# Moving the late copies of row maxima, and the score units, in a transformer layer on one core

## The chip, the cores and the metric

One of the cores of a Trainium2 chip runs the whole program. The metric is the device time of one execution in microseconds (us), as a median over runs. The core has five engines that each work through their own list of instructions in order and wait for each other by semaphores: PE (TensorE, matrix products; PEld is its loading of weights), DVE (VectorE), ACT (ScalarE), POOL (GpSimd) and SP (SyncE, which here issues the DMAs).

## The reference

A layer over 4 batches of 512 tokens with 256 features: causal attention with 16 heads, and a gated feed forward with 1024 hidden features. Cut to what matters:

```python
qkv = layernorm(x) @ w_qkv.T + b_qkv            # q, k get a rotary embedding
attn = softmax(where(causal, -inf, q @ k.T * HEAD_DIM ** -0.5))
x = x + layernorm((attn @ v) @ w_out.T + b_out)
h = layernorm(x)
hidden = fwht(silu(h @ W1.T) * (h @ W3.T))      # Walsh-Hadamard transform
x = x + layernorm(hidden @ W2.T)
```

All is float32, and the kernel keeps nearly that precision: most products are made of three products of high and low halves.

## The kernel before, in words

The softmax needs the largest score of each query row before the exponential. So the scores are computed twice. In a first pass, **score units** (`score_unit` on PE, ACT, POOL and DVE) compute scores with queries on the partitions, for one tile of 128 queries (qt, 0 to 3) and as many heads as fit 512 columns. DVE (line 923) takes the maximum of each row. When all heads of a tile are done, ACT copies the maxima as their high half (line 688), POOL (`max_low`, line 811) makes the low half, a unit of kind "turn" lets PE transpose both (line 430), and ACT copies the rows into `q_t` (line 677), twice for each turn. There are 44 units of scores and 5 turns: units 0 to 41 run inside the feed forward of the batch before (for the first batch, ahead of everything), and the last 7, the **tail** (the last six heads of the last query tile, and their turn), run inside the attention of the batch itself.

In the second pass, `attend`, PE computes scores again with keys on the partitions (`score_t`, line 448, four matmuls for a head) and the maxima are subtracted in the same product. ACT takes the exponential of a head (`exps`, line 656, 128x1280), POOL zeroes the masked triangle (`cut`, lines 820 and 823), and PE multiplies with the values (`values`, line 464), four heads to a group, in four steps by key tile. `values(g, kt)` starts six heads behind `score_t`. In one pass of `attend`'s loop PE does `score_t(h)`, then the tail units that `TAIL_AFTER[h]` names, then a step of `values`. Heads and units are counted from 0 here.

Score units use the banks of `ps` in turn; in the feed forward these are banks 4 and 5, so a unit waits until the unit two places earlier has had its maxima taken, or, where that was a turn, until ACT has made both of its row copies. In the tail, units use banks 6 and 7; `values` of group 0 writes to bank 6 and of group 1 to bank 7.

The feed forward runs over 8 chunks of hidden features (a = 0 to 7). For each PE does four `up` products, ACT the silu (line 662), DVE the product with the second half (`gate`, line 1001), ACT the high half (`hid_high`, line 668), POOL the low half (`hid_low`, line 803), and PE four `down` products for the chunk before. `UNITS_AFTER` is a table with a row for each chunk: how many score units go between its ups, how many between the downs that follow, and how many ahead of the last chunk's downs (`gap`). Each engine goes through the same list of steps. Units that the table leaves over come behind the last down.

ACT needs another table of functions for exp than for silu. A one-element exponential (line 714) loads it ahead of time.

On POOL, the iteration of a batch is: `cut` of all 16 heads; behind head 5 (`ROOT_AFTER`) the reciprocal root for the next batch's layer norm (`root(b + 1, "x")`, line 779, which waits for DVE's statistics, line 879); and the `max_low` of the tail where the table says. DVE works through the six tail maxima, then the last subtractions of the batch before, and then the statistics of x for the next batch.

Of the kernel before, what the change touches and what calls it, by code (L numbers as in the profile page):

```python
# [30 lines left out]
ACT = mybir.ActivationFunctionType  # L31
# [7 lines left out]
HCH = HIDDEN // P  # L39
# [27 lines left out]
N_SCORES = len(UNITS)  # L67
# [4 lines left out]
TAIL_UNITS = range(N_UNITS, len(UNITS))  # L72
SCORE_NO = [sum(u[0] == "scores" for u in UNITS[:n]) for n in range(len(UNITS))]
TAIL_BANKS = [6 + n % 2 for n in range(TAIL)] + [7]
TAIL_AFTER = {4: (0, 2), 5: (2, 4), 6: (4, 6), 7: (6, 7)}


def turn_of(unit):
# [60 lines left out]

UNITS_AFTER = [(0, 0, 0), (3, 2, 0), (2, 3, 0), (4, 1, 0), (4, 2, 0), (4, 3, 0), (4, 3, 0), (4, 1, 0), (0, 0, 1)]
STEPS, EARLY_UNITS = feed_forward_steps(UNITS_AFTER)
STEPS_LAST, _ = feed_forward_steps(None)
UNIT_BANKS = unit_banks(EARLY_UNITS)
FIRST_UNIT_BANKS = [4 + n % 4 for n in range(N_UNITS - 1)] + [5] + TAIL_BANKS
# [13 lines left out]
def layer_kernel(nc, x, w_qkv, b_qkv, w_out, b_out, w1, w3, w2, rope, hadamard, eye, mask, selector, out):  # L160
    ctx = ExitStack()
    with ctx:
# [72 lines left out]
        minus_half = sb("minus_half", [P, TILES])  # L235
        spare = sb("spare", [P, 1])
# [135 lines left out]
        def _(pe):  # L372
# [79 lines left out]
            def values(b, g, kt):  # L452

                if kt == 0:
                    if g == 0:
                        pe.wait_ge(S["maxed"], (b + 1) * N_SCORES)
                    pe.wait_ge(S["masked"], b * HEADS + 4 * g + 4)
                    if g == 1:
                        pe.wait_ge(S["rows_in"], 2 * (b + 1) * N_TURNS)
                    if g >= 2:  # L460
                        pe.wait_ge(S["o_copied"], b * GROUPS + g - 1)
                for j in range(4):
                    h = 4 * g + j
                    ins = pe.matmul(ps[32 * j:32 * j + 32, 6 + g % 2, kt * P:TOKENS], v_t[:, kt, h, :],  # L464
                                    probs[:, h % PROBS, KEY_COL[kt]:KEY_COL[kt] + TOKENS - kt * P],
                                    start=(kt == 0), stop=(kt == TILES - 1), skip_group_check=True)
                if kt == TILES - 1:
                    ins.then_inc(S["pv_done"], 1)
# [158 lines left out]
        def _(act):  # L627
# [30 lines left out]
            def silu(b, a):  # L658
                act.wait_ge(S["up_done"], b * HCH + a + 1)
                if a >= 2:  # L660
                    act.wait_ge(S["hid_l"], b * HCH + a - 1)
                act.activation(gate[:, a % 2, :], bank(2 * (a % 2)), ACT.Silu).then_inc(S["silu_done"], 1)  # L662
# [44 lines left out]
            def feed_forward(b, steps):  # L707
                for kind, n, i in steps:
                    if kind == "up" and i == 3:
                        silu(b, n)  # L710
                    elif kind == "gate":
                        hid_high(b, n)
                        if n == HCH - 1:
                            act.activation(spare[:, :], minus_half[:, 0:1], ACT.Exp)
                    elif kind == "unit":
                        score_unit(b + 1, n, UNIT_BANKS)

# [37 lines left out]
            def iteration(b, order, steps):  # L755
                for h in range(HEADS):
                    exps(b, h)
                    for n in range(*TAIL_AFTER.get(h + 1, (0, 0))):
                        score_unit(b, TAIL_UNITS[n], UNIT_BANKS if b else FIRST_UNIT_BANKS)
                if order is MIX:  # L760
                    for t in range(TILES):
                        xt_high(b + 1, t)
                mix(b, order)
                feed_forward(b, steps)
# [8 lines left out]
        def _(pool):  # L773
# [32 lines left out]
            def max_low(b, n):  # L806
                turn = turn_of(UNITS[n])
                if turn is not None:
                    qt, first, stop = TURNS[turn]
                    pool.wait_ge(S["max_h"], b * N_TURNS + turn + 1)  # L810
                    pool.tensor_tensor(max_s[:, qt % 2, 1, first:stop], maxima[:, qt % 2, first:stop],
                                       max_s[:, qt % 2, 0, first:stop].bitcast(F32), ALU.subtract).then_inc(S["max_l"], 1)
# [13 lines left out]
            def iteration(b, order, steps):  # L826
                for h in range(HEADS):
                    cut(b, h)
                    for n in range(*TAIL_AFTER.get(h + 1, (0, 0))):
                        max_low(b, TAIL_UNITS[n])  # L830
                    if h == ROOT_AFTER and order is MIX:
                        root(b + 1, "x")
                for m in order:
                    if m[0] == "e":
                        rope_products(b + 1, int(m[1]))
                    elif m[0] in "vw":
                        root(b, {"v": "y", "w": "h"}[m[0]] + m[1])
                for kind, n, i in steps:
                    if kind == "gate":
                        hid_low(b, n)  # L840
                    elif kind == "unit":
                        max_low(b + 1, n)
                    elif kind == "ln_z":
                        root(b, "z%d" % i)
# [284 lines left out]
```

## Time and profile before

| | |
|---|---|
| median of 3 runs | 500.91 us (500.86 to 501.76) |
| the profiled execution, its own time | 497.78 us |
| its span in the profile | 496.1 us |
| PE busy with matmuls | 405.0 us (82% of the span) |
| DVE busy | 281.2 us (57%) |
| ACT busy | 210.9 us (43%) |
| POOL busy | 162.1 us (33%) |
| mean granted TensorE clock | 0.938 |

The four batches follow each other at some 107 us. Attention of the second batch runs from about 189 to 218 us in the span, then comes a mixed stage (output projection, normalisation, and q, k, v of the next batch), and the rest of the period is feed forward, with the score units of the next batch among it. PE is the busiest engine in all of them, so what counts is where PE waits.

### The profile page before, as it was taken

The numbers are of one execution on the slowest core, as the hardware profiler recorded it, in microseconds if no ns is written. First come the engines' busy times: TensorE is split into PE (matmuls) and PEld (weight loads), VectorE is DVE, ScalarE is ACT, GpSimd is POOL, SyncE is SP. The second block draws the span as 40 slices with busy tenths as digits, with TensorE's granted clock in tenths as the row PEclk, the third lists the DMA queues.
The fourth block names the chain that finished last, engine by engine and source line by source line (L and its number), as shares of the span: only waits on it lengthen the run. The fifth ranks groups of instructions, "written<-read, shape, count | busy, mean of one in ns | idle before, by whom it ended". The sixth has DMA issues, their size and how long they took to land.

```text
span 496.1 us, 7892 instructions
## 1 busy us (share of the span) xinstructions
PE 405.0 (82%) x2884; PEld 338.2 (68%) x2884; DVE 281.2 (57%) x936; ACT 210.9 (43%) x314; POOL 162.1 (33%) x284
## 2 busy tenths in 40 slices
PE   1679677999599997988599988987799979858992
PEld 1569645558489985557499975566699965448991
DVE  7554583625937776536856776267576754273114
ACT  4445234753323337843423347813332367423221
POOL 4136002533512226514422235614132245321232
PEclk9999865999969999999889999999799999997998
DMA  6549900000397000200695001102880002000001
GB/s 230 215 136 247 212 1 1 2 2 0 127 255 171 1 1 1 85 1 1 179 245 130 1 1 42 44 1 72 219 201 21 1 1 85 1 1 1 1 1 42
DMA packets 35463, 36.95 MB, mean 74 GB/s; under 512 B 2016, under 2 KB 34528, under 8 KB 35424
## 3 DMA queue, kind: packets, MB, share of 16 engines
q1 hardware_dynamic: 35424, 36.45, 26.6%
q8 instruction: 23, 0.38, 0.3%
q14 instruction: 16, 0.13, 0.1%
HBM read 21.76 MB, written 14.68 MB: 73 GB/s over the span
## 4 chain that ended last, share of the span: by engine, by line
PE 58%; DVE 13%; DMA 9%; issue 7%; ACT 6%; SPq 3%; POOL 2%; DVEq 0%; POOLq 0%; ACTq 0%
PE ps L266 30%; PE ps L448 8%; PE ps L464 7%; PE ps L436 5%; DMA qk_scratch<-qk_s 4%; DMA q_t<-qk_scratch 4%; ACT probs L656 4%; DVE masked_scores L923 2%; SPq L293 2%; DMA raw_bias<-in_b_out 2%; PE ps L498 2%; DVE xy L985 1%; POOL hid_s L803 1%; PE ps L405 1%; DVE stats_h L870 1%
## 5 line engine op out<-in xcount | busy, mean ns | idle before, releaser
L923 DVE CUSTOM_DVE_ANT_0 masked_scores<-ps,mask_row 128x128 bf16<-128x128 f32 (+3 forms) x256 | 114.4, 488 | 61.6 <-PE ps L436 61.1
L266 PE MATMUL ps<-xt,w_s 128*128 128x256 f32 x768 | 111.7, 294 | 0.0
L266 PEld LDWEIGHTS ps<-xt,w_s 128*128 128x128 f32 x768 | 106.2, 202 | 0.5
L803 POOL TENSOR_TENSOR hid_s<-gate,hid_s 128x512 fp32r<-128x512 f32 x32 | 41.2, 1287 | 135.9 <-ACT hid_s L668 135.9
L656 ACT ACTIVATE probs<-ps 128x1280 f32<-128x1280 f32 x64 | 76.4, 1242 | 9.5 <-PE ps L448 8.9
L436 PE MATMUL ps<-k_t,q_t 96*128 96x128 f32 (+3 forms) x256 | 71.7, 356 | 9.8 <-DMA q_t<-qk_scratch 5.6
L448 PEld LDWEIGHTS ps<-q_t,k_t 128*128 128x128 f32 x256 | 44.9, 198 | 32.2 <-ACT probs L656 14.7
L266 PE MATMUL ps<-w_s,hid_s 128*128 128x256 f32 x384 | 55.5, 284 | 7.0 <-POOL hid_s L803 7.0
L448 PE MATMUL ps<-q_t,k_t 128*128 128x512 f32 (+3 forms) x256 | 55.7, 345 | 5.6 <-ACT probs L656 4.0
L266 PEld LDWEIGHTS ps<-w_s,hid_s 128*128 128x128 f32 x384 | 51.6, 190 | 9.3 <-POOL hid_s L803 8.7
L436 PEld LDWEIGHTS ps<-k_t,q_t 96*128 96x128 f32 x256 | 43.0, 198 | 18.6 <-DVE maxima L923 10.9
L464 PE MATMUL ps<-probs,v_t 128*32 128x128 f32 (+3 forms) x512 | 43.6, 441 | 4.8 <-DVE maxima L923 3.9
L662 ACT ACTIVATE gate<-ps 128x512 f32<-128x512 f32 x32 | 19.1, 596 | 64.1 <-PE ps L266 64.0
L1001 DVE TENSOR_TENSOR gate<-gate,ps 128x512 f32<-128x512 f32 x32 | 21.9, 685 | 41.9 <-ACT gate L662 41.7
L266 PE MATMUL ps<-wqkv_s,q_t 128*128 128x512 f32 (+1 forms) x192 | 41.8, 356 | 3.6 <-DVE bias_s L1061 3.6
L820 POOL TENSOR_SCALAR_AFFINE_SELECT probs<-probs 128x384 f32<-128x384 f32 x64 | 33.8, 528 | 31.7 <-ACT probs L656 31.4
L797 POOL TENSOR_TENSOR rot_s<-qk_b,rope_t 128x256 f32<-128x256 f32 x32 | 25.7, 824 | 49.6 <-ACT qk_b L646 41.2
L930 DVE COPY o_t<-ps 128x512 f32<-128x512 f32 x16 | 11.1, 692 | 49.5 <-PE ps L464 49.0
L266 PEld LDWEIGHTS ps<-wqkv_s,q_t 128*128 128x128 f32 x192 | 32.3, 200 | 8.6 <-issue 4.0
L668 ACT ACTIVATE hid_s<-gate 128x512 fp32r<-128x512 f32 x32 | 20.2, 631 | 29.3 <-DVE gate L1001 29.3
L630 ACT ACTIVATE xt<-ps 128x256 fp32r<-128x256 f32 x32 | 12.0, 384 | 44.5 <-PE ps L507 33.0
L405 PE MATMUL ps<-ident,rot 128*128 128x128 f32 x64 | 11.6, 309 | 21.6 <-DVE rot L910 21.6
(99 smaller groups left out, 485.3 us busy)
## 6 DMA issues: line engine op xcount, KB each, us to landing
qk_scratch<-qk_s SPq DMA_DIRECT2D x32, 256.0 KB, 5.6
k_t<-qk_scratch SPq DMA_DIRECT2D x16, 384.0 KB, 5.5
q_t<-qk_scratch SPq DMA_DIRECT2D x8, 768.0 KB, 8.8
qk_scratch<-qk_s SPq DMA_DIRECT2D x8, 512.0 KB, 5.5
xa<-in_x SPq DMA_DIRECT2D x4, 512.0 KB, 9.6
xy<-in_x SPq DMA_DIRECT2D x4, 512.0 KB, 3.5
out<-xy SPq DMA_DIRECT2D x8, 256.0 KB, 2.3
o_t<-in_w SPq DMA_DIRECT2D x1, 1024.0 KB, 10.0
```

The costliest lines, as they stand in the source:

```text
L266: ins = eng.matmul(o, lhs(i), rhs(j), start=first and n == 0, stop=last and n == 2, skip_group_check=skip)
L436: ins = pe.matmul(o[:, i * keys:(i + 1) * keys], q_t[0:QK_ROWS, h // 2, qt * P:qt * P + P], k_t[0:QK_ROWS, h, 0:keys], start=(i == 0), sto ...
L448: ins = pe.matmul(ps[:, col // 512, col % 512:col % 512 + n], k_t[:, h, kt * P:kt * P + P], q_t[:, h // 2, kt * P:TOKENS], start=(kt != 3) ...
L464: ins = pe.matmul(ps[32 * j:32 * j + 32, 6 + g % 2, kt * P:TOKENS], v_t[:, kt, h, :], probs[:, h % PROBS, KEY_COL[kt]:KEY_COL[kt] + TOKENS ...
L656: act.activation(probs[:, h % PROBS, :], src, ACT.Exp, scale=SCALE).then_inc(S["exp_done"], 1)
L662: act.activation(gate[:, a % 2, :], bank(2 * (a % 2)), ACT.Silu).then_inc(S["silu_done"], 1)
L668: act.activation(hid_s[:, a % 2, 0, :], gate[:, a % 2, :], ACT.Copy).then_inc(S["hid_h"], 1)
L797: ins = pool.tensor_tensor(o[:, :, e, :], src[:, :, 1 - e, :], tab[:, 1, e, :].unsqueeze(1).broadcast_to([P, 2 * HEADS, HALF]), ALU.mult)
L803: pool.tensor_tensor(hid_s[:, a % 2, 1, :], gate[:, a % 2, :], hid_s[:, a % 2, 0, :].bitcast(F32), ALU.subtract).then_inc(S["hid_l"], 1)
L820: pool.affine_select(out=v, in_=v, compare_op=ALU.is_ge, fill=0.0, base=0, pattern=[[0, 3], [1, P]], channel_multiplier=-1)
L923: ins = dve.tensor_tensor_reduce(masked_scores[:, SCORE_NO[n] % 2, i * keys:(i + 1) * keys], ps[:, banks[n], i * keys:(i + 1) * keys], mas ...
L1001: dve.tensor_tensor(gate[:, n % 2, :], gate[:, n % 2, :], bank(2 * (n % 2) + 1), ALU.mult)\
```

## The change

Six edits belong together. On PE, the tail's turn goes from behind `score_t(7)` to behind `score_t(8)`. On ACT and POOL, the copy of the last six heads' maxima goes from behind head 5 to behind head 7, and ACT's copy of their rows from behind head 6 to behind head 8. `values` of group 0 waits for one maximum less: for five of the six tail units. In the feed forward, two units go from behind the last chunk's ups to the chunks before, and the turn of the first ten heads goes from behind the last down to ahead of the last chunk's downs. ACT loads its table for exp ahead of the last `hid_high`, not behind it.

```diff
-TAIL_AFTER = {4: (0, 2), 5: (2, 4), 6: (4, 6), 7: (6, 7)}
+TAIL_AFTER = {4: (0, 2), 5: (2, 4), 6: (4, 6), 8: (6, 7)}
+TAIL_COPY_AFTER = {7: 5, 8: 6}
...
-UNITS_AFTER = [(0, 0, 0), (3, 2, 0), (2, 3, 0), (4, 1, 0), (4, 2, 0), (4, 3, 0), (4, 3, 0), (4, 1, 0), (0, 0, 1)]
+UNITS_AFTER = [(0, 0, 0), (3, 2, 0), (2, 3, 0), (4, 1, 0), (4, 2, 0), (4, 4, 0), (4, 4, 0), (4, 0, 0), (0, 0, 1)]
...
                     if g == 0:
-                        pe.wait_ge(S["maxed"], (b + 1) * N_SCORES)
+                        pe.wait_ge(S["maxed"], (b + 1) * N_SCORES - 1)
...
                     if kind == "up" and i == 3:
                         silu(b, n)
+                        if n == HCH - 1:
+                            act.activation(spare[:, :], minus_half[:, 0:1], ACT.Exp)
                     elif kind == "gate":
                         hid_high(b, n)
-                        if n == HCH - 1:
-                            act.activation(spare[:, :], minus_half[:, 0:1], ACT.Exp)
...
                     exps(b, h)
-                    for n in range(*TAIL_AFTER.get(h + 1, (0, 0))):
-                        score_unit(b, TAIL_UNITS[n], UNIT_BANKS if b else FIRST_UNIT_BANKS)
+                    if h in TAIL_COPY_AFTER:
+                        score_unit(b, TAIL_UNITS[TAIL_COPY_AFTER[h]], UNIT_BANKS if b else FIRST_UNIT_BANKS)
...
                     cut(b, h)
-                    for n in range(*TAIL_AFTER.get(h + 1, (0, 0))):
-                        max_low(b, TAIL_UNITS[n])
+                    if h in TAIL_COPY_AFTER:
+                        max_low(b, TAIL_UNITS[TAIL_COPY_AFTER[h]])
```

The first place is POOL in the attention of the first batch. AFFINE_SELECT rows are `cut`, two for each head, rstd_x and shift_x are the root for the next batch, and max_s is `max_low` of the last six heads. Before, from the end of head 5's cut:

```order
L823 AFFINE_SELECT probs<-probs 128x128
L811 TENSOR_TENSOR max_s<-maxima,max_s 128x6
L779 TENSOR_TENSOR rstd_x<-mv_x,minus_half 128x4
L782 TENSOR_TENSOR shift_x<-mv_x,rstd_x 128x4
L820 AFFINE_SELECT probs<-probs 128x3x128
```

And in the changed kernel (its lines are one higher), from the same instruction:

```order
L824 AFFINE_SELECT probs<-probs 128x128
L780 TENSOR_TENSOR rstd_x<-mv_x,minus_half 128x4
L783 TENSOR_TENSOR shift_x<-mv_x,rstd_x 128x4
L821 AFFINE_SELECT probs<-probs 128x3x128
L824 AFFINE_SELECT probs<-probs 128x128
L821 AFFINE_SELECT probs<-probs 128x3x128
L824 AFFINE_SELECT probs<-probs 128x128
L812 TENSOR_TENSOR max_s<-maxima,max_s 128x6
```

`max_low` stood ahead of the root; now it stands behind it and behind the cuts of heads 6 and 7.

The second place is PE in the feed forward: the downs that follow the ups of chunk 6 (rows with hid_s), up to the first up of chunk 7. L436 is a score unit, L430 the turn of query tile 2 (unit 34). Before:

```order
L436 MATMUL ps<-k_t,q_t 128x512
L266 MATMUL ps<-w_s,hid_s 128x256 x6
L436 MATMUL ps<-k_t,q_t 128x512
L266 MATMUL ps<-w_s,hid_s 128x256 x3
L436 MATMUL ps<-k_t,q_t 128x512
L266 MATMUL ps<-w_s,hid_s 128x256 x3
L430 MATMUL ps<-ident_r,max_s 32x128
L266 MATMUL ps<-xt_65,w_s 128x256 x6
```

In the changed kernel:

```order
L437 MATMUL ps<-k_t,q_t 128x512
L267 MATMUL ps<-w_s,hid_s 128x256 x3
L437 MATMUL ps<-k_t,q_t 128x512
L267 MATMUL ps<-w_s,hid_s 128x256 x3
L431 MATMUL ps<-ident_r,max_s 32x128
L267 MATMUL ps<-w_s,hid_s 128x256 x3
L437 MATMUL ps<-k_t,q_t 128x512
L267 MATMUL ps<-w_s,hid_s 128x256 x3
L437 MATMUL ps<-k_t,q_t 128x512
L267 MATMUL ps<-xt_65,w_s 128x256 x6
```

The turn came last before the ups; now two units follow it, and the second of them (unit 36) uses the turn's bank.

The third place is ACT from the silu of chunk 7 to the first exponentials. Before:

```order
L662 ACTIVATE gate<-ps 128x512
L668 ACTIVATE hid_s<-gate 128x512
L714 ACT_TABLE_LOAD
L714 ACTIVATE spare<-minus_half 128x1
L688 ACTIVATE max_s<-maxima 128x10
L677 ACTIVATE q_t<-ps 32x128
L677 ACTIVATE q_t<-ps 32x4x128
L656 ACTIVATE probs<-ps 128x1280 x6
```

In the changed kernel:

```order
L663 ACTIVATE gate<-ps 128x512
L713 ACT_TABLE_LOAD
L713 ACTIVATE spare<-minus_half 128x1
L689 ACTIVATE max_s<-maxima 128x10
L669 ACTIVATE hid_s<-gate 128x512
L678 ACTIVATE q_t<-ps 32x128
L678 ACTIVATE q_t<-ps 32x4x128
L657 ACTIVATE probs<-ps 128x1280 x8
```

The table load and the copy of the first ten heads' maxima now stand between the silu and the last `hid_high`.

## Rows read from the trace of the kernel before

**Rows 1.** Timeline, second batch's attention: start us, us, engine, line, idle before.

```profile
198.28 0.08 DVE L923 DVE_READ_ACCUMULATOR2_ANT maxima<- 128x1 f32 x1
...
198.89 0.08 DVE L923 DVE_READ_ACCUMULATOR2_ANT maxima<- 128x1 f32 x1
...
199.03 1.07 PE L464 MATMUL ps<-probs,v_t 128*32 128x512 f32 x8 [0.98 <-DVE maxima L923]
...
201.90 1.01 POOL L779 TENSOR_TENSOR rstd_x<-mv_x,minus_half 128x4 f32<-128x4 f32 x1 [2.34 <-DVE mv_x L879]
...
202.44 0.64 PE L464 MATMUL ps<-probs,v_t 128*32 128x256 f32 x8
...
203.14 0.52 POOL L820 TENSOR_SCALAR_AFFINE_SELECT probs<-probs 128x384 f32<-128x384 f32 x1
...
204.59 0.53 POOL L820 TENSOR_SCALAR_AFFINE_SELECT probs<-probs 128x384 f32<-128x384 f32 x1
```

**Rows 2.** Timeline ahead of the first batch's attention: a low half, then its turn.

```profile
79.19 0.21 POOL L811 TENSOR_TENSOR max_s<-maxima,max_s 128x10 fp32r<-128x10 f32 x1 [5.89 <-ACT max_s L688]
...
79.55 0.27 PE L430 MATMUL ps<-ident_r,max_s 128*32 128x128 f32 x1 [2.22 <-POOL max_s L811]
```

**Rows 3.** Timeline, first batch's attention (94 to 96) and the last one's.

```profile
94.67 0.52 POOL L820 TENSOR_SCALAR_AFFINE_SELECT probs<-probs 128x384 f32<-128x384 f32 x1
...
95.03 0.64 PE L464 MATMUL ps<-probs,v_t 128*32 128x256 f32 x8
...
415.94 4.83 ACT L656 ACTIVATE probs<-ps 128x1280 f32<-128x1280 f32 x4
...
416.85 0.64 PE L464 MATMUL ps<-probs,v_t 128*32 128x256 f32 x8
...
417.34 0.52 POOL L820 TENSOR_SCALAR_AFFINE_SELECT probs<-probs 128x384 f32<-128x384 f32 x1 [1.66 <-ACT probs L656]
```

**Rows 4.** The chain that ended last, in order of time: start us, us, what.

```profile
173.06 0.18 PE ps L436
173.24 0.35 PE ps L266 x3
```

**Rows 5.** Timeline, feed forward of the first batch, chunks 5 to 7.

```profile
173.55 0.19 PEld L436 LDWEIGHTS ps<-k_t,q_t 96*128 96x128 f32 x1 [0.16 <-DVE maxima L923]
...
179.05 0.63 ACT L668 ACTIVATE hid_s<-gate 128x512 fp32r<-128x512 f32 x1 [0.97 <-DVE gate L1001]
...
179.75 0.94 PE L266 MATMUL ps<-xt,w_s 128*128 128x256 f32 x6
...
179.95 1.06 ACT L677 ACTIVATE q_t<-ps 32x128 fp32r<-32x128 f32 x2 [0.27 <-PE ps L430]
...
183.58 0.60 ACT L662 ACTIVATE gate<-ps 128x512 f32<-128x512 f32 x1 [2.56 <-PE ps L266]
...
185.15 0.63 ACT L668 ACTIVATE hid_s<-gate 128x512 fp32r<-128x512 f32 x1 [0.97 <-DVE gate L1001]
...
185.80 1.28 ACT L714 ACT_TABLE_LOAD   x1
...
187.18 1.68 PE L266 MATMUL ps<-w_s,hid_s 128*128 128x256 f32 x12 [1.49 <-POOL hid_s L803]
187.20 0.20 ACT L688 ACTIVATE max_s<-maxima 128x10 fp32r<-128x10 f32 x1
...
188.70 0.22 PE L430 MATMUL ps<-ident_r,max_s 128*32 128x128 f32 x1
...
189.28 1.50 PE L448 MATMUL ps<-q_t,k_t 128*128 128x512 f32 x8 [0.35 <-ACT q_t L677]
```

**Rows 6.** Timeline, last batch's feed forward, chunk 7.

```profile
484.53 0.63 ACT L668 ACTIVATE hid_s<-gate 128x512 fp32r<-128x512 f32 x1 [0.75 <-DVE gate L1001]
```

**Rows 7.** Stretches of the first mixed stage (busy by engine, PEclk, DMA), then PE's timeline.

```profile
134.00:136.00 2.00, 0.00 (x0) 0.00 (x0) 1.99 (x4) 1.72 (x3) 1.44 (x2) 0.65 0.56 195
...
136.22 1.11 PE L405 MATMUL ps<-ident,rot 128*128 128x128 f32 x4 [2.62 <-DVE rot L910]
```

## The prediction

> **What bounds the kernel now.** The page says that PE is the busiest engine (82% of the span), so I looked for the places where PE waits, in the timeline around each edit, and read from the chain which of those waits reach the end of the program. Two places matter: the middle of each attention, and the end of each feed forward.
>
> In the second batch's attention [rows 1] the reader is to see PE waiting 0.98 us at 199.03 for DVE's last tail maximum, which ends at 198.97, before `values(0,0)`. From there the chain runs on PE alone through the rest of the attention but for its last exponential: score products and value products follow each other without a gap. Whatever delays PE there delays the end by as much. The same rows show POOL: its root for the next batch waits for DVE's statistics until 201.90, takes 1.01, and `cut(6)` starts only at 203.14. `cut(6)` and `cut(7)` together take 1.45 (203.14 to 204.59). Before the change nobody cared: POOL had made the low half of the tail maxima ahead of the root.
>
> At the end of the feed forward [rows 5] PE waits 1.49 us for the low half of chunk 7 (187.18), behind silu, gate, high half and low half in a row. Then the turn of the first ten heads (188.70) and ACT's copy of its rows hold up the first `score_t` until 189.28.
>
> **The change, part by part.** *`values` wait for five of the six tail units.* The fifth unit's maximum is read at 198.28 + 0.08, the sixth's at 198.89 + 0.08 [rows 1]. PE starts `values(0,0)` 0.61 sooner, at 198.42. ACT no longer stands still for the maxima, so exponential 6 starts with its scores. That gives -0.6 per batch if nothing else comes in the way.
>
> *The tail's turn, its low half behind the root and two cuts.* POOL's list is now cut 5, root, cut 6, cut 7, `max_low`. The root's time is set by DVE's statistics, which DVE makes behind the sixth maximum, as before. So the cuts stay at 203.14 and `max_low` starts at 204.59. From the start of a `max_low` to its turn on PE it took 79.55 - 79.19 = 0.36 [rows 2]: the turn comes at 204.95. I allow 0.15 for the turn, so `values(0,2)`, which stands behind it in PE's list with everything after, starts at 205.10. Before it started at 202.44 [rows 1]. That is +2.66, with the 0.61 already in it: PE would be there at 198.42 + 3.41 = 201.83, and waits some 3.1 us. Behind PE's wait for the turn stand `values(0,2)`, `score_t(9)` and all later heads. ACT needs 4.83 us for four heads [rows 3] and is not what the chain runs over there, so it has nothing to give back.
>
> The first batch: `cut(6)` at 94.67 [rows 3], + 1.45 + 0.36 + 0.15 = 96.63 against 95.03: +1.6. The third batch has the pattern of the second: +2.7. The last batch has no root. There exponential 7 can start about 1.1 before its 415.94 (0.6 from the values, 0.5 since it no longer stands behind the row copies), its cut 1.40 later (417.34 - 415.94), then 0.8 for the cut, 0.36 and 0.15: 417.5 against 416.85 [rows 3], so +0.6. Sum for the attentions: 1.6 + 2.7 + 2.7 + 0.6 = +7.6. The row copies behind exponential 8 are made long before `score_t(10)` needs them; were that cover gone, they would cost their 0.5 us a batch.
>
> *Two units earlier in the feed forward.* They leave PE's idle stretch ahead of chunk 7's downs, where they cost nothing, for chunks 5 and 6, where PE has no gap. In chunk 5, unit 27 starts at 173.55 when DVE has freed its bank [rows 5], and will again, but now a down (0.35) and a unit (0.18) [rows 4] follow it: +0.5, and nearly 0.1 for a wider unit among the ups of chunk 6. In chunk 6, the turn of tile 2 came last before the ups. Now units 35 and 36 follow it and unit 36 uses its bank, so it waits for ACT's two row copies (1.06 us), which stand behind `hid_high(6)`: 179.05 + 0.6 + 0.63 + 1.06 = 181.3 [rows 5]. With the unit itself (0.24, estimated from the chain's other units) the ups of chunk 7 start at 181.6, not at 179.75: +1.85.
>
> *The exp table ahead of `hid_high(7)`.* From the load's start to ACT's next work it took 187.20 - 185.80 = 1.40 [rows 5]. Now that and the maxima's copy (0.2) stand between silu and `hid_high`. Before, 185.15 - (183.58 + 0.60) = 0.97 lay there, for the gate. So +0.6 on the chain to the downs. In the last batch there is no maxima's copy, and 0.75 lay there [rows 6]: +0.65, to the very end.
> The Trainium skill (ScalarE: Activation LUTs, "What ACT_TABLE_LOAD costs") has 1283 ns for the load, as here, and about 1380 ns for a drain besides. The row shows no such drain: the spare exponential and the next copy follow in 1.40 in all. By the page each of four moves would cost 1.4 more, 5.5 in the sum; by the row nothing. I take the row.
>
> *The turn of ten heads ahead of the downs.* It now falls into PE's idle stretch, and its row copies are done while the downs run. `score_t(0)` can start where the turn was, at about 188.65 instead of 189.28 [rows 5]: -0.65.
>
> Per feed forward with units (three): 1.85 + 0.6 - 0.65 = +1.8, in all +5.4.
>
> **Sum.** 7.6 + 5.4 + 0.65 = +13.6 us. Against the profiled execution's own 497.78 this gives 511.4; the median of the runs is 500.91, 3.1 above it, and I add to the median: 514.5. No transfer is on these paths; output and input DMAs shift with the batches.
>
> **The clock.** In the first mixed stage the granted clock fell from 1.0 (2.4 GHz) to 0.5 (1.2 GHz) in a stretch without PE work, 2.62 us idle before a matmul [rows 7]. PE's 1.49 us wait at 187.18 cost no clock. The new waits of about 3.1 us (second and third batch) lie near the first. I take it that one of the two brings such a fall, and price it at 1.6 us: some 3 us of work that PE bounds at half speed. Bounds: nothing, and 3.4 for a fall of double length. So 516 us.
>
> **Rivals.** (1) *The clock falls in most of the new gaps*: the attentions of three batches and the ends of three feed forwards, where PE's idle stretch grows from 1.5 to over 2.5. Six falls at 1.6 are 9.6, so 524. For it: gaps near 2.6. Against: PE's work stands close on both sides. Chance 0.12.
> (2) *The bank waits in the feed forward are hidden*: if chunk 6 doesn't wait for the row copies, its +1.85 shrinks to the two units, 0.5; -1.3 three times, and without the clock: 514.5 - 4 = 510.5. The waits are in the program by bank and order, so against it speaks all but the exact times. Chance 0.11.
> (3) *Faster.* The change wins if POOL reaches `max_low` before PE reaches the turn, so that no new wait comes. Then attention gains 0.6 four times, the early turn 0.65 three times, the table load costs 0.6 four times and the units 0.5 three times: near -0.5; with the load hidden too, -2.9, so 498. The place is POOL's root: it would have to start by 201.83 - 0.36 - 1.45 - 1.24 = 198.8; the row has 201.90, for statistics that DVE can't begin before the sixth maximum. Chance 0.04.
> (4) *No change*: the delays are taken up by slack behind them. PE is the chain to the end of each attention. Chance 0.03.
> (5) *A drain at each table load*, as worked out above from 1.4 four times: with the rest, 521.5. Ruled out nearly by 187.20 - 185.80. Chance 0.03.
> The forecast keeps 0.67.
>
> **How the numbers follow.** The forecast's own range is 512 to 519 (clock from nothing to three falls, and 2 us of error over seven terms). To hold 8 in 10 it is stretched toward (2) and part of (1): 509.5 to 521. Within 0.2% (1 us) is about what a measurement can't tell from no change. Slower: 0.67 + 0.12 + 0.11 + 0.03 = 0.93; same 0.03; faster 0.04.
>
> **What the profile after would show.** Right: PE's turn in the attention of batches two and three with an idle time near 3 us before it, released by POOL's `max_s`, about 2 in the first and 1 in the last; POOL's `max_s` of 128x6 behind the second cut after the root; `values(0,0)` with an idle time of some 0.4; a wait of unit 36 on ACT's `q_t` of 0.5 us or more in chunk 6; ACT's table load directly behind the silu, with `hid_high(7)` about 2.1 behind silu's start; `score_t(0)` directly behind the last downs. Wrong: `max_s` done before PE gets to the turn; a root that doesn't wait for statistics; or a drop of the granted clock in each attention.

## The result, and the profile after

| | before | changed |
|---|---|---|
| median of 4 runs | 500.88 us | 520.32 us (518.13 to 522.08) |
| ratio, 95% interval | | 1.0394 (1.0338 to 1.0451) |
| span of the profiled execution | 496.1 us | 519.3 us |
| mean granted TensorE clock | 0.938 | 0.921 |

The changed kernel is 19.4 us slower; 516 was forecast, within 509.5 to 521. Run again beside other kernels (below) it was 18.2 us slower (517.22 against 499.01, ratio 1.0356, 1.0316 to 1.0396).

The first view is the timeline of the changed kernel in the second batch's attention, the place of [rows 1]:

```profile
204.86 0.08 DVE L924 DVE_READ_ACCUMULATOR2_ANT maxima<- 128x1 f32 x1
...
205.00 1.07 PE L465 MATMUL ps<-probs,v_t 128*32 128x512 f32 x8 [0.38 <-DVE maxima L924]
...
208.50 1.01 POOL L780 TENSOR_TENSOR rstd_x<-mv_x,minus_half 128x4 f32<-128x4 f32 x1 [3.93 <-DVE mv_x L880]
...
209.73 0.52 POOL L821 TENSOR_SCALAR_AFFINE_SELECT probs<-probs 128x384 f32<-128x384 f32 x1
...
211.20 0.20 POOL L812 TENSOR_TENSOR max_s<-maxima,max_s 128x6 fp32r<-128x6 f32 x1
...
211.55 0.22 PE L431 MATMUL ps<-ident_r,max_s 128*32 128x128 f32 x1 [3.14 <-POOL max_s L812]
211.70 1.06 PE L465 MATMUL ps<-probs,v_t 128*32 128x256 f32 x8
```

`values(0,0)` now waits 0.38 us where it waited 0.98. Then comes the new wait: the turn (PE, L431) waits 3.14 us for the low half (`max_s`), which POOL makes behind the root and two cuts. From the start of `max_low` to the turn lie 0.35 us, from the turn to `values(0,2)` 0.15. The same view of the other batches has this wait at 2.09, 3.14 and 0.95 us; the forecast had 2, 3, 3 and 1.

Next the timeline at the end of the first batch's feed forward, the place of [rows 5]:

```profile
184.19 0.50 PE L437 MATMUL ps<-k_t,q_t 96*128 96x512 f32 x1 [0.55 <-DVE maxima L924]
184.22 1.06 ACT L678 ACTIVATE q_t<-ps 32x128 fp32r<-32x128 f32 x2
...
185.33 0.50 PE L437 MATMUL ps<-k_t,q_t 96*128 96x512 f32 x1 [0.28 <-ACT q_t L678]
...
189.43 0.60 ACT L663 ACTIVATE gate<-ps 128x512 f32<-128x512 f32 x1 [4.15 <-PE ps L267]
...
190.05 1.28 ACT L713 ACT_TABLE_LOAD   x1
...
191.34 0.20 ACT L713 ACTIVATE spare<-minus_half 128x1 f32<-128x1 f32 x1
...
191.55 0.61 ACT L669 ACTIVATE hid_s<-gate 128x512 fp32r<-128x512 f32 x1
...
192.08 0.22 PE L431 MATMUL ps<-ident_r,max_s 128*32 128x128 f32 x1 [1.03 <-POOL max_s L812]
...
193.56 2.04 PE L267 MATMUL ps<-w_s,hid_s 128*128 128x256 f32 x12 [1.27 <-POOL hid_s L804]
...
195.41 2.44 PE L449 MATMUL ps<-q_t,k_t 128*128 128x512 f32 x8
```

Unit 36 waits for ACT's row copies, as forecast, but only 0.28 us; unit 35 in front of it waits 0.55 for DVE's maxima. Together with the units themselves they put the silu of chunk 7 13.83 us behind that of chunk 5, where it was 11.90: 1.93 more. The table load stands directly behind the silu, and the high half starts 2.12 us after the silu (before: 1.57). The turn of ten heads sits in PE's gap, which it splits in two (1.03 and 1.27).

What was not forecast is the length of the last two rows: 12 products took 1.68 us before and take 2.04 here, and two heads of scores 2.44 and not 1.50. The view by stretches of the changed kernel shows why (PEclk is the number behind the engines' busy times):

```profile
98.00:102.00 4.00, 4.00 (x32) 2.18 (x24) 2.20 (x5) 2.48 (x4) 0.87 (x3) 0.64 0.02 4
194.00:198.00 4.00, 3.85 (x19) 3.46 (x17) 3.07 (x12) 1.29 (x2) 1.92 (x5) 0.59 0.02 4
211.00:215.00 4.00, 3.45 (x22) 1.99 (x23) 0.22 (x1) 1.36 (x3) 1.12 (x4) 0.60 0.28 98
307.00:311.00 4.00, 3.21 (x14) 3.17 (x15) 1.40 (x6) 0.30 (x1) 1.00 (x2) 0.57 0.00 0
327.00:331.00 4.00, 4.00 (x25) 2.12 (x24) 2.19 (x5) 2.43 (x2) 0.85 (x2) 0.60 0.01 4
423.00:427.00 4.00, 4.00 (x18) 3.87 (x19) 2.44 (x11) 0.34 (x1) 1.24 (x4) 0.57 0.00 0
```

Behind each of six new or longer gaps of PE (three attentions, three ends of a feed forward) the granted clock went to 0.5 (1.2 GHz) for most of these four microseconds. None of the six places has such a fall in the kernel before. The changed kernel's second profile (below) has six falls at the same places.

To see what each stage costs I took three kinds of marks from the timelines: the first `score_t` of a batch, the first transposition of the next x, and the silu of chunk 5. Lengths in us:

| stage | before | changed | changed, gaps filled (below) |
|---|---|---|---|
| attention of batch 1 (first) | 26.29 | 28.73 | 28.80 |
| attention of batches 2, 3 | 24.78, 24.78 | 29.36, 28.99 | 27.37, 27.37 |
| from silu of chunk 5 to the next `score_t` (3 times) | 17.60, 17.61, 17.61 | 19.81, 20.69, 20.36 | 19.53, 19.54, 19.53 |
| mixed stage to silu of chunk 5 (3 times) | 65.03, 64.29, 65.34 | 64.84, 65.05, 65.49 | 64.90, 64.63, 65.52 |
| attention of the last batch, to its first output transposition | 28.89 | 29.82 | 29.26 |

Nothing was lost or won in the mixed stages, which the change doesn't touch, beyond their scatter. Two readings of this table need care. The first attention starts while the clock is still at half from what stands before it: for its first 6.4 us in the kernel before, 3.5 in the changed one and 9.4 in the filled one, so its three lengths can't be compared as they stand. And a fall at the end of a feed forward can reach into the next attention: the one of the first batch (194.7 to 198.1) lies mostly behind the `score_t` at 195.41, so that attention 2 has the slow time of two falls.

### The profile page after: what moved, and what is told of

The parts are those of the page before. It is cut to its first block, busy times and chain, and to the rows that moved or that the text cites. A ratio compares the mean times of both kernels' runs of the same rounds, so it can differ in the third digit from the quotient of the medians.

```text
span 519.3 us, 7892 instructions
## 1 busy us (share of the span) xinstructions
PE 413.8 (80%) x2884; PEld 343.5 (66%) x2884; DVE 282.1 (54%) x936; ACT 210.7 (41%) x314; POOL 161.6 (31%) x284
## 4 chain that ended last, share of the span: by engine, by line
PE 51%; DVE 13%; DMA 13%; issue 8%; ACT 7%; SPq 4%; POOL 4%; POOLq 0%; DVEq 0%; ACTq 0%
PE ps L267 26%; PE ps L449 7%; PE ps L465 6%; DMA q_t<-qk_scratch 6%; DMA qk_scratch<-qk_s 6%; PE ps L437 5%; ACT probs L657 4%; SPq L294 2%; DVE masked_scores L924 2%; DMA raw_bias<-in_b_out 2%; PE ps L499 1%; DVE xy L986 1%; POOL hid_s L804 1%; PE ps L406 1%; DVE stats_h L871 1%
## 5 line engine op out<-in xcount | busy, mean ns | idle before, releaser
L437 PE MATMUL ps<-k_t,q_t 96*128 96x128 f32 (+3 forms) x256 | 73.1, 360 | 15.4 <-DMA q_t<-qk_scratch 7.6
L449 PEld LDWEIGHTS ps<-q_t,k_t 128*128 128x128 f32 x256 | 47.4, 209 | 33.0 <-ACT probs L657 17.3
L267 PE MATMUL ps<-w_s,hid_s 128*128 128x256 f32 x384 | 59.0, 294 | 7.0 <-POOL hid_s L804 7.0
L449 PE MATMUL ps<-q_t,k_t 128*128 128x512 f32 (+3 forms) x256 | 58.2, 356 | 4.2 <-ACT probs L657 3.6
L267 PEld LDWEIGHTS ps<-w_s,hid_s 128*128 128x128 f32 x384 | 54.4, 198 | 8.4 <-POOL hid_s L804 7.8
L465 PE MATMUL ps<-probs,v_t 128*32 128x128 f32 (+3 forms) x512 | 46.1, 463 | 2.4 <-DVE maxima L924 1.5
```

Of the source, the lines that this page charges most:

```text
L267: ins = eng.matmul(o, lhs(i), rhs(j), start=first and n == 0, stop=last and n == 2, skip_group_check=skip)
L437: ins = pe.matmul(o[:, i * keys:(i + 1) * keys], q_t[0:QK_ROWS, h // 2, qt * P:qt * P + P], k_t[0:QK_ROWS, h, 0:keys], start=(i == 0), sto ...
L449: ins = pe.matmul(ps[:, col // 512, col % 512:col % 512 + n], k_t[:, h, kt * P:kt * P + P], q_t[:, h // 2, kt * P:TOKENS], start=(kt != 3) ...
```

## The experiments

Each was timed in five rounds beside the kernel before; its ratio is against the same chip's runs of it. The microseconds are differences of two medians. The ratios are not the quotients of these medians and can differ from them by 0.2 to 0.3% (idle work in the attention's gap: 13.3 us, or 14.5 by the ratio), so a difference of a microsecond between two kernels is not to be read from them. First the change's parts alone, then its repairs.

**The attention alone.** The changed kernel with the table of units and the table load of before.

```diff
-UNITS_AFTER = [(0, 0, 0), (3, 2, 0), (2, 3, 0), (4, 1, 0), (4, 2, 0), (4, 4, 0), (4, 4, 0), (4, 0, 0), (0, 0, 1)]
+UNITS_AFTER = [(0, 0, 0), (3, 2, 0), (2, 3, 0), (4, 1, 0), (4, 2, 0), (4, 3, 0), (4, 3, 0), (4, 1, 0), (0, 0, 1)]
```

> Only the edits in the attention (turn, copies, and the values' wait); table of units and the exp table load as before. Theory A (waits and clock): the three new waits of PE cost 7.6 us as forecast, and each of the three long ones brings a fall of the clock worth some 1.2 us more: +11.2 us, and the clock at half in the middle of three attentions. Theory B (waits alone, the rest of the loss lies in the feed forward): +7.6 us and no falls there.

Measured 511.56 against 498.56: +13.0 us, ratio 1.0248 (1.0209 to 1.0288). Attention of batches 2 and 3 took 29.97 and 30.16 us, 5.2 and 5.4 more than before; with 2.7 for the wait, 2.5 and 2.7 are left. The view by stretches of this kernel, with the clock at 0.59 over seven microseconds:

```profile
205.00:212.00 7.00, 4.79 (x29) 3.02 (x33) 1.49 (x4) 2.24 (x5) 3.41 (x11) 0.59 0.23 75
```

The first attention shows no fall and is 1.2 us longer (27.45, with 4.9 us at half clock at its start, against 6.4). So theory A holds, but with two falls and not three, each twice as long, and twice as dear, as I had priced it (1.2 us).

**The table of units alone.**

```diff
-UNITS_AFTER = [(0, 0, 0), (3, 2, 0), (2, 3, 0), (4, 1, 0), (4, 2, 0), (4, 3, 0), (4, 3, 0), (4, 1, 0), (0, 0, 1)]
+UNITS_AFTER = [(0, 0, 0), (3, 2, 0), (2, 3, 0), (4, 1, 0), (4, 2, 0), (4, 4, 0), (4, 4, 0), (4, 0, 0), (0, 0, 1)]
```

> Only the table of score units (two units earlier, turn of ten heads ahead of the last downs). Both theories: the silu of chunk 7 some 1.9 us later, score_t(0) 0.65 nearer to the last downs, so +1.25 us for each of three feed forwards, +3.8 us. Theory A: PE's idle time ahead of the last downs stays near 1.5 us, so no fall of the clock there. Theory B: falls there too, +6 us or more.

Measured 504.82 against 498.56: +6.3 us, ratio 1.0110 (1.0075 to 1.0146). Theory A had the clock wrong here. The stage from silu 5 to `score_t` took 20.10, 18.97 and 20.00 us: +1.4 in the one where the clock stayed up (1.25 was expected), and 2.5 and 2.4 in the two where it fell. The gap and what follows it in the first batch, in the timeline:

```profile
190.04 2.89 PE L266 MATMUL ps<-w_s,hid_s 128*128 128x256 f32 x12 [1.75 <-POOL hid_s L803]
```

The gap stands at 1.75, since two units have left it (1.49 before), and the 12 products behind it take 2.89 and not 1.68. This kernel had a third fall, at 91.1, in the first attention, whose instructions and waits are those of the kernel before; it came behind the old wait of `values(0,0)`:

```profile
91.02 1.88 PE L464 MATMUL ps<-probs,v_t 128*32 128x512 f32 x8 [0.98 <-DVE maxima L923]
```

**The table load alone.**

```diff
                     if kind == "up" and i == 3:
                         silu(b, n)
+                        if n == HCH - 1:
+                            act.activation(spare[:, :], minus_half[:, 0:1], ACT.Exp)
```

> Only the exp table load ahead of the last high half. By the row of 1.40 us: +0.6 us in each of four feed forwards, +2.4 us. By a drain of 1.4 us at each load: +8 us. If the load were hidden behind the gate: 0.

Measured 504.04 against 498.56: +5.5 us, ratio 1.0099 (1.0066 to 1.0132). ACT's timeline rules out a drain: the load starts 0.01 us behind the silu's end and takes 1.28, and the next instruction starts with its end.

```profile
181.88 0.60 ACT L662 ACTIVATE gate<-ps 128x512 f32<-128x512 f32 x1 [2.56 <-PE ps L266]
182.49 1.28 ACT L712 ACT_TABLE_LOAD   x1
183.78 0.20 ACT L712 ACTIVATE spare<-minus_half 128x1 f32<-128x1 f32 x1
183.89 0.61 ACT L668 ACTIVATE hid_s<-gate 128x512 fp32r<-128x512 f32 x1
```

The high half starts 2.01 behind the silu, 0.44 later than before (the maxima's copy still stands behind it here). Three times that and 0.67 in the last batch are 2.0. The rest, 3.5 us, goes with the clock, as far as one profile shows it: it fell behind the first and second end of a feed forward, and not behind the third (a gap of 1.94 there), but then behind the 0.98 us wait of `values(0,0)` in the last attention, a wait that the kernel before has too, without a fall (the table of units alone had one there, in its first attention). By stretches and in the timeline:

```profile
186.00:191.00 5.00, 4.45 (x21) 3.77 (x21) 3.51 (x13) 1.73 (x3) 2.15 (x7) 0.66 0.01 3
```

```profile
415.44 1.88 PE L464 MATMUL ps<-probs,v_t 128*32 128x512 f32 x8 [0.98 <-DVE maxima L923]
```

So a gap that grows by half a microsecond seems to have cost more through the clock than by itself; the last batch's two stages were 3.3 us longer than before in this profile (30.40 and 65.31 against 28.89 and 63.52), of which the load explains 0.7. The parts don't add up: 1.0248, 1.0110 and 1.0099 make 4.6% together, the change 3.6 to 3.9%. Units and load each bring falls at the feed forwards' ends, and together there is still one fall at each. That this makes the difference was not tried, and the difference, 0.6 to 1.0%, is about as large as the uncertainty of the four ratios together.

**The shorter wait of the values alone.**

```diff
                     if g == 0:
-                        pe.wait_ge(S["maxed"], (b + 1) * N_SCORES)
+                        pe.wait_ge(S["maxed"], (b + 1) * N_SCORES - 1)
```

> Only the values' wait for one maximum less; turn and copies stand where they stood before. Theory A: the one part of the change that gains: values(0,0) 0.6 us sooner in each of four attentions, -2.4 us, since POOL makes the low half ahead of the root. Rival: exponential 6 still stands behind the maxima's copy on ACT and takes the gain back: 0.

Measured 495.97 against 498.56: -2.6 us, ratio 0.9957 (0.9928 to 0.9985). This is the gaining part of the change, hidden under the rest. That the number matches the expected -2.4 is partly luck: by the stages the gain is 0.28 us in the second attention (24.50) and 0.62 in the last (28.27), not 0.6 in each. In the second, PE gives back 0.3 us when it comes to `values(1,0)` too early for POOL's cut of head 7, which stands behind the root:

```profile
206.39 1.07 PE L464 MATMUL ps<-probs,v_t 128*32 128x512 f32 x8 [0.29 <-POOL probs L823]
```

The profiled execution was the slowest of twelve (501.24). Its third attention had a fall (from 302.6), and with it took 25.65. Ahead of this fall PE had only waits that the kernel before has too: 1.49 at the end of the feed forward, some 7 us earlier, and then 0.35, 0.68, 0.28 and 0.26.

```profile
302.00:306.00 4.00, 3.74 (x12) 3.32 (x13) 1.31 (x4) 3.08 (x4) 2.32 (x7) 0.57 0.00 0
```

**The root behind head 8.** Only `ROOT_AFTER` of the changed kernel is altered.

```diff
-ROOT_AFTER = 5
+ROOT_AFTER = 8
```

> The changed kernel with POOL's root for the next batch behind head 8's cut, not behind head 5's, so that the low half of the late maxima no longer stands behind it. If the root in POOL's queue is what holds up PE's turn: the wait falls from 3.1 (2.1 in the first batch) to the 0.95 that the last batch has, so 5.5 us less wait, and the clock stays up in the middle of the attentions: 7 to 9 us less than the changed kernel, some 12 us above the kernel before. If ACT's or the exponentials' order were the cause, the wait stays near 3 us and nothing changes (+19).

Measured 509.01 against 499.08: +9.9 us, ratio 1.0179 (1.0129 to 1.0230), where the changed kernel itself has 1.0356 and 1.0394. The timeline of the second batch:

```profile
205.62 0.29 POOL L824 TENSOR_SCALAR_AFFINE_SELECT probs<-probs 128x128 f32<-128x128 f32 x1
205.89 0.20 POOL L812 TENSOR_TENSOR max_s<-maxima,max_s 128x6 fp32r<-128x6 f32 x1
...
206.23 0.22 PE L431 MATMUL ps<-ident_r,max_s 128*32 128x128 f32 x1 [0.95 <-POOL max_s L812]
```

The wait is 0.95 in all four batches, as in the last before, and no clock falls behind it. The root in POOL's queue made two of the three microseconds (one of two in the first batch). The rest is `max_low`'s place behind cut 7, as the order of the rows has it; no run moves that alone. Of the three ends of a feed forward, which are those of the changed kernel, only the third had a fall; the first was followed by one 4.6 us into the next attention (196.3), the second by none.

**Idle work in the attention's gap.**

```diff
                     for n in range(*TAIL_AFTER.get(h, (0, 0))):
+                        if n == TAIL and ahead:
+                            pe.wait_ge(S["maxed"], (b + 1) * N_SCORES)
+                            for _ in range(FILL[b]):
+                                pe.matmul(ps[:, 7, 0:256], ident_r[:, :], q_t[:, 0, 0:256],
+                                          start=True, stop=True, skip_group_check=True)
```

> The changed kernel with idle work for PE in the new gap of the attention: 16 matmuls of 256 columns (25 in batches two and three) that multiply constants into a bank nobody reads, 0.107 us each, ahead of the wait for the turn. Theory A (the gap itself makes the clock fall): the clock stays at 2.4 GHz in these three places, the turn comes at the same time, and the program is 3 to 5 us faster than the changed kernel (+15 or +16 over before). Theory B (the falls there cost nothing): no difference, +19.

Measured 512.36 against 499.08: +13.3 us, ratio 1.0291 (1.0243 to 1.0338). The second attention, which in this run had no fall, took 27.57 us: 2.8 over before, where I had forecast 2.7 for the waits. (A fall at the feed forward's end reached 0.5 us into it.) The third had a fall 4.6 us behind its first `score_t` (312.1, 28.53 us), far ahead of the filled gap; whether it belongs to the feed forward's end is not shown. The time itself, 13.3 us over before by the medians and 14.5 by the ratio, came out somewhat under the expected 15 or 16. The matmuls multiply the unit matrix with `q_t`, not with constants as expected above; nobody reads the product.

**Idle work in all six gaps, beside the changed kernel itself.** The same, and 8 and 10 such matmuls, on `wo_s` into bank 0, ahead of the turn of ten heads and ahead of the last chunk's downs.

```diff
                     elif kind == "down":
+                        if n == HCH - 1 and i == 0 and b < BATCHES - 1:
+                            idle_work(10)
                         down(b, n, i)
                     elif kind == "unit":
+                        if n == N_UNITS - 1:
+                            idle_work(8)
                         score_unit(b + 1, n, UNIT_BANKS)
```

> The changed kernel with idle work for PE in all six new gaps: in the attentions as in the fill run, and 8 and 10 matmuls in the 1.0 and 1.3 us of PE's gap at the end of each feed forward with units. Theory A (each of six falls costs 1.0 to 1.8 us): the falls are gone at the feed forwards' ends too, and what is left is the waits as forecast, +13 to +14 us against the kernel before, 6 to 7 less than the changed kernel, 1 to 3 less than the fill of the attentions alone. Theory B (the falls there cost nothing): as with the fill of the attentions alone.

> The changed kernel itself, so that it stands on the same chip as the others of this call. By its first measurement +19.4 us.

Measured, on one chip: 513.79 with idle work (ratio 1.0280, 1.0247 to 1.0313) and 517.22 without (1.0356, 1.0316 to 1.0396), against 499.01. The timeline and two of the stretches of the filled kernel:

```profile
206.20 3.21 PE L488 MATMUL ps<-q_t,ident_r 128*128 128x256 f32 x25
209.49 0.22 PE L432 MATMUL ps<-ident_r,max_s 128*32 128x128 f32 x1
```

```profile
192.00:196.00 4.00, 3.26 (x24) 2.82 (x22) 2.29 (x11) 1.32 (x2) 1.51 (x5) 1.00 0.00 0
208.00:214.00 6.00, 5.92 (x53) 3.84 (x56) 2.18 (x5) 2.98 (x4) 3.34 (x10) 1.00 0.29 90
```

All six falls are gone, and the stages become equal among batches (27.37, 27.37; 19.53, 19.54, 19.53). Against the changed kernel's first profile that is 1.99 + 1.62 in the attentions and 0.28 + 1.16 + 0.83 at the feed forwards' ends, 5.9 us; the medians give 3.4 us. The two need not disagree: by the intervals of the two ratios the difference is anything from about 1 to 6 us. Besides, the profiled run of the filled kernel was longer behind the last attention (65.7 against 64.1 us), where the clock falls at other places from run to run.

**One unit moved back.**

```diff
-UNITS_AFTER = [..., (4, 4, 0), (4, 4, 0), (4, 0, 0), (0, 0, 1)]
+UNITS_AFTER = [..., (4, 4, 0), (4, 3, 0), (4, 1, 0), (0, 0, 1)]
```

> The changed kernel with one unit of chunk 6's downs moved back behind chunk 7's downs ((4,4) (4,3) (4,1), so unit 36 stands behind an up and not between the downs). If unit 36's wait for ACT's row copies and its bank makes most of the 1.9 us in chunk 6: the silu of chunk 7 comes some 1 us sooner in each of three feed forwards, but the turn of ten heads has a maximum less time: in all 1 to 3 us faster than the changed kernel. If only the number of units counts: 0.25 us for each, under 1 us.

Measured 514.84 against 499.08, ratio 1.0302 (1.0256 to 1.0348), which the changed kernel's interval overlaps: unclear by the medians. By the stages it is clear: 18.71, 18.72 and 18.70 us against 19.53 without a fall, 0.8 less each time. The silu of chunk 7 comes 0.95 sooner (12.88 behind that of chunk 5, not 13.83), as expected if the waits count and not the number of units. But the turn of ten heads, whose maxima now come later, waits 2.43.

**Only what gains: the copies behind the exponentials, POOL's order as before.** The kernel before with the values' shorter wait, and on ACT alone:

```diff
+ACT_COPY_AFTER = {6: 5, 7: 6}
...
                     exps(b, h)
-                    for n in range(*TAIL_AFTER.get(h + 1, (0, 0))):
-                        score_unit(b, TAIL_UNITS[n], UNIT_BANKS if b else FIRST_UNIT_BANKS)
+                    if h in ACT_COPY_AFTER:
+                        score_unit(b, TAIL_UNITS[ACT_COPY_AFTER[h]], UNIT_BANKS if b else FIRST_UNIT_BANKS)
```

> The kernel before, with the values' shorter wait and only ACT's copies moved (maxima behind exponential 6, rows behind exponential 7); the turn on PE, POOL's low half ahead of the root, the table of units and the table load stay as before. values(0,0) starts 0.6 us sooner and exponential 6 doesn't stand behind the maxima: -2.4 us as with the shorter wait alone if ACT has slack there, and up to 1 us more if ACT was the limit. Rival: PE's turn comes to wait for the low half, since the copy is 1.2 us later behind exponential 6: 0 or slower.

Measured 496.63 against 499.08: -2.5 us, ratio 0.9956 (0.9930 to 0.9981), no more than the shorter wait alone. The last attention gained 0.61 us (28.28), the second and third only 0.27 (24.51). The timeline of the second shows who took the rest, the root again, through the cuts behind it:

```profile
197.89 1.06 PE L465 MATMUL ps<-probs,v_t 128*32 128x512 f32 x8 [0.37 <-DVE maxima L924]
...
204.16 1.06 PE L465 MATMUL ps<-probs,v_t 128*32 128x512 f32 x8 [0.27 <-POOL probs L824]
```

**The same with the root behind head 8.**

```diff
-ROOT_AFTER = 5
+ROOT_AFTER = 8
```

> The kernel with the shorter wait of the values and ACT's copies behind exponentials 6 and 7, and POOL's root behind head 8's cut. With the root behind head 5 that kernel gained 0.61 in the last attention but only 0.27 in the second and third, where values(1,0) waited for POOL's cut 7, 0.27 us at 204.16. If the root in POOL's queue takes that away: 0.3 us more in each of three attentions, -3.3 us in all against the kernel before. Rival: the root, now later, holds up the cuts behind it or the normalisation: no gain over -2.4, or a loss.

Measured 496.54 against 499.01: -2.5 us, ratio 0.9955 (0.9927 to 0.9982). The stages show what was expected (24.16, 24.15 and 28.25 us, so 0.62 to 0.64 less than before in each), but another third of a microsecond in each of three attentions is below what the medians tell. These two kernels, and the shorter wait alone, beat the kernel before by 0.4 to 0.5%, with intervals clear of 1, and the changed one by far.

**Idle work in the old gaps.**

```diff
+MIX_FILL = {"r2": 11, "r3": 21, "H0": 0}
...
+                    if b >= 0 and m in MIX_FILL and (order is MIX or m == "H0"):
+                        if order is MIX:
+                            pe.wait_ge(S["qk_copied"], (b + 1) * TILES + 3)
+                        fill(MIX_FILL[m] if order is MIX else 40)
```

> The same, and 11 and 21 idle matmuls of PE in the two gaps of each mixed stage (1.5 and 2.6 us, waits for DVE's rotation) and 40 in the last one's 5 us gap. The kernel before has a fall of the clock behind each of them (6.8 to 10.2 us at half). If the gaps cause the falls: the clock stays up there, and what lies behind is bound by PE only in part (a DMA wait lies in it), so 1 to 1.5 us in each of four stages: -7 to -9 us against the kernel before. Rival: the DMA wait swallows it: same as without, -3.3.

Measured 500.38 against 499.01, ratio 1.0009 (0.9976 to 1.0042): no gain, and rather a loss against its base, the kernel of the section before (0.9955). The stretch of the first mixed stage, first before, then with idle work:

```profile
129.00:145.00 16.00, 10.86 (x54) 9.71 (x53) 9.61 (x25) 5.67 (x11) 4.70 (x8) 0.68 0.84 225
```

```profile
129.00:145.00 16.00, 12.81 (x97) 11.60 (x96) 10.03 (x26) 6.55 (x13) 5.27 (x8) 1.00 0.85 221
```

The clock went from 0.68 to 1.00 over 16 us, and the stage took 64.77 us (65.03 before, 64.68 in its base). What PE gains it waits away at the first score unit of the next batch, for the DMA of `q_t`, where the kernel before and the base had no wait for it:

```profile
145.88 0.66 PE L438 MATMUL ps<-k_t,q_t 96*128 96x128 f32 x4 [2.29 <-DMA q_t<-qk_scratch]
```

So there the DMA sets the pace, and half the clock costs nothing. The third mixed stage was 1.9 us longer than in the base (67.14 against 65.22), with 3.12 us of this wait; why the DMA came later there is open.

## Why the prediction was right, and where it was short

*The values' shorter wait*: right where it stands. 0.61 sooner was forecast, and `values(0,0)` waits 0.38 where it waited 0.98. Alone it is worth 2.6 us by the medians, but by the stages only 0.28 in an attention with a root and 0.62 in the last. In the changed kernel it is no gain at all in the attentions: PE only comes sooner to its wait for the turn.

*The tail's turn behind root and cuts*: right in place and size. Forecast +1.6, +2.7, +2.7, +0.6 with waits of 2 to 3 us; measured waits 2.09, 3.14, 3.14, 0.95, and with the clock up +2.6 in the second and third attention, +0.4 in the last. The first attention is less sure: it came out 1.2 to 3.0 longer in the kernels with this order, and the clock at its start differs among runs. The two at 1.2 had about 1.5 us less at half clock there than the kernel before. So 1.6 is neither refuted nor shown. That the root is the cause and not ACT's order is shown by moving the root alone (0.95 us of wait).

*Two units earlier, the table load, the early turn*: forecast +1.8 for each feed forward; with the clock up it was +1.9 (19.53 against 17.61). The units gave 1.93 (forecast 1.85) with waits at units 35 and 36. The prediction had named a wait of 0.5 or more at unit 36 as its sign; it was 0.28, since unit 35 had already waited 0.55. The early turn gave back 0.57 (forecast 0.65): the units' table alone made the stage only 1.36 longer where the clock stayed up. The load's part was 0.55 against a forecast of 0.6, and 0.67 in the last batch against 0.65. The drain of some 1.4 us that the Trainium skill adds to a load (ScalarE: Activation LUTs, "What ACT_TABLE_LOAD costs") doesn't appear: the load's end and the next start are 0.01 us apart (182.49 + 1.28, 183.78). By such a drain rival 5 gave 521.5, near the measured time for a reason that is not there.

*The clock*: this step failed. "I take it that one of the two brings such a fall, and price it at 1.6 us" met six falls, three of them at the ends of feed forwards. Rival 1, the falls in most of the new gaps, is what happened; I gave it 0.12. With it came one of the signs that the prediction had named for being wrong, a drop of the clock in the attentions (in three of four). The price of one fall was not far off: against the filled kernel's 27.37 and 19.53, a stage with one fall of some three and a half microseconds took 1.0 to 1.7 us longer, one with a fall of twice that 2.4 to 2.8 (forecast 1.6 and 3.4). Six at 1.6, rival 1's 9.6 us, was too much: 5.9 by the stages of the first profile, 3.4 by medians.

*The sum.* The filled kernel, without the six falls, stands 14.8 us above the kernel before. Its stages show where: 2.51, 2.59, 2.59 and 0.37 in the attentions, 1.93, 1.93 and 1.92 at the ends of the feed forwards, and the load's 0.67 in the last batch make 14.5 (the first attention with a longer slow start). The forecast had 13.6 for this, and 1.6 for the clock where 3.4 to 5.9 was measured. So the time lies in the stated range partly by luck: the mechanism that the forecast kept had 512 to 519, and 520.3 is outside it (the second measurement's 18.2 us would make 519.1); it is inside 521 only since the range was stretched toward rival 1.

*The other rivals*: the bank waits were not hidden, nothing was taken up by slack. The faster rival named the right place: with POOL's low half ahead of the root there is a gain, though only half of it until the root moves behind the cuts.

## What to carry to other kernels

Moving an instruction later on one engine moves it past what stands there: ask for each queue what the thing is now behind, and when that ends. Here a gain of 0.3 us for an attention was real and could be had by leaving POOL's order alone, and 0.6 by moving the root behind head 8 as well; with the copy behind a root that waits for statistics the same step cost 2.7. And price a new gap of TensorE twice, once as a wait and once for the clock behind it: but only where TensorE bounds what follows.

## What was not expected of the hardware

Whether the clock falls behind a gap is not a matter of its length alone, nor the same in every run of the same instructions:

- Gaps of 3.14 and 2.09 us in the attentions had a fall behind them each time in the changed kernel's two profiles; with the attention's edits alone, and with one unit moved back, the gap of the first batch had none (2.09 and 2.06 us), and three of the four others had falls of twice the length.
- Two gaps of 1.03 and 1.27 with one short transposition between them had a fall behind them in all three batches in both profiles of the changed kernel. With the root moved, or the attention's gap filled, the same place had one directly behind it in one of three batches each.
- Gaps of some 1.75 us (the table of units alone) were followed by a fall in two of three places. The gap of 1.49 never was in the kernel before, and in the run of the values' shorter wait a fall came 7 us behind it once.
- The 0.98 us wait of `values(0,0)` had a fall behind it twice, in the first attention of the units' run and in the last of the table load's.

So a single profile doesn't tell which of two kernels gets more falls. What the idle work shows is firmer, though from one profile too: with all six gaps filled, none of the six places had a fall, where the changed kernel had six in each of its two.

The price of one fall of some three and a half microseconds was 1.0 to 1.7 us in places that TensorE bounds, and none in the mixed stage, where a DMA bounds. Matmuls that nobody reads kept the clock at 2.4 GHz behind the six new gaps and behind the first three mixed stages' gaps (a fall in the third came only behind a DMA wait of 3.12 us, further on); in the last mixed stage a shorter fall remained. Where the gap was a wait anyway they put nothing on the path: the turn of the second batch came 15.6 us behind the attention's first `score_t` with them, and 15.7 without (the attention's edits alone).
